# Three expert tiles of a step as one group, in the first layer of a two-layer RWKV / mixture-of-experts kernel

## The reference

```python
# s: RWKV, a recurrence over the 256 tokens of each sequence and channel
k, v, r = xk @ W_k.T, xv @ W_v.T, sigmoid(xr @ W_r.T)
wkv_t = (e1 * aa + e2 * v_t) / (e1 * bb + e2 + 1e-9)      # aa, bb, pp: carried from token to token
s = (r * wkv) @ W_o.T
# f: one of 8 experts for each token
xn  = rms_norm(x) * scale
ids = argmin(dist2(xn, centroids))
h   = xn @ up_w[e];  a, g = split(h)                       # up_w[e]: 128 x 512
y   = (a * silu(g)) @ down_w[e]                            # down_w[e]: 256 x 128
f   = where(ids == e, y, out) + x
```

## Time and profile before

| what | value |
|---|---|
| median of three runs | 1186.43 us (1185.88 to 1188.76) |
| span of the profiled execution | 1199.2 us |
| PE busy | 1061.0 us, 88% of the span |
| DVE busy | 957.6 us, 80% |
| ACT busy | 868.2 us, 72% |
| POOL busy | 789.8 us, 66% |
| DMA, mean | 89 GB/s |
| mean granted TensorE clock | 0.936 of 2.4 GHz |

### The profile page before, as it was taken

The page is one execution under the profiler, slowest core; times in us unless marked ns, Lnnn a source line. Parts: engine busy times, 40 slices in busy tenths (PEclk is TensorE's granted clock), DMA queues, the critical chain, the costliest instruction groups (busy, mean ns, idle before and its releaser), DMA issues.

```text
span 1199.2 us, 29232 instructions
## 1 busy us (share of the span) xinstructions
PE 1061.0 (88%) x8890; PEld 711.9 (59%) x8890; DVE 957.6 (80%) x2144; ACT 868.2 (72%) x2186; POOL 789.8 (66%) x1147
## 2 busy tenths in 40 slices
PE   2666369999986799999999999999999999999986
PEld 1545258898874455565555565556555565556643
DVE  6768989999994687878878887888787887888861
ACT  2555248877772488888888888888888788888874
POOL 4476678787883556776667766776677666776631
PEclk9766679999996699999999999999999999999988
DMA  9411135555552223322333233322332232323310
GB/s 258 101 39 37 34 88 162 149 156 158 143 146 67 59 69 89 86 74 66 93 79 85 65 80 82 93 68 71 90 87 73 66 89 78 90 66 77 84 33 11
DMA packets 158400, 106.17 MB, mean 89 GB/s; under 512 B 74216, under 2 KB 138408, under 8 KB 158120
## 3 DMA queue, kind: packets, MB, share of 16 engines
q1 hardware_dynamic: 154152, 95.80, 30.8%
q0 software_dynamic: 4096, 8.53, 2.5%
HBM read 72.69 MB, written 31.47 MB: 87 GB/s over the span
## 4 chain that ended last, share of the span: by engine, by line
PE 52%; issue 5%; ACT 4%; DVE 4%; DMA 2%; SPq 1%; POOL 1%; another core or an unknown queue 0%; DVEq 0%; POOLq 0%
PE PS L1956 8%; PE PS L1946 6%; PE PS L2021 5%; PE PS L1928 5%; PE PS L2043 5%; ACT PT L1802 4%; PE PS L2035 3%; DVE bm L1592 3%; PE PS L1998 3%; PE PS L2008 3%; PE PS L1898 3%; PE PS L1970 3%; PE PS L1986 3%; PE PS L2052 2%; PE PS L1906 1%
## 5 line engine op out<-in xcount | busy, mean ns | idle before, releaser
L1592 DVE TENSOR_REDUCE bm<-PS 128x16 f32<-128x1024 f32 x256 | 312.4, 1220 | 35.4 <-PE PS L1928 28.4
L1802 ACT ACTIVATE PT<-PS 128x1024 f32<-128x1024 f32 x256 | 262.0, 1024 | 23.8 <-PE PS L1946 20.4
L1956 PE MATMUL PS<-PT,rows 128*32 128x256 f32 x2048 | 138.6, 388 | 2.2 <-ACT OT L1807 2.2
L1481 POOL TENSOR_TENSOR Pr<-Pr,linv 128x512 f32<-128x512 f32 x128 | 131.6, 1039 | 5.0
L1776 ACT ACTIVATE Pr<-PS,nmf 128x256 f32<-128x256 f32 x256 | 117.1, 473 | 0.3 <-DVE nmf L1612 0.3
L1612 DVE TENSOR_REDUCE nmf<-PS 128x4 f32<-128x1024 f32 x64 | 78.4, 1225 | 46.7 <-PE PS L2021 46.7
L1946 PE MATMUL PS<-QS,KS 51*128 51x256 bf16 x1024 | 100.0, 274 | 12.3 <-ACT PT L1802 5.4
L1928 PE MATMUL PS<-KS,QS 48*128 48x256 bf16 x1024 | 101.5, 277 | 9.5 <-DVE bm L1592 6.4
L482 POOL DMA_INDIRECT xs_dram<-rows,slot x64 | 65.3, 1021 | 40.5 <-DVEq L715 22.8
L1021 PE MATMUL PS<-S,wmix 128*128 128x256 f32 x192 | 69.4, 448 | 17.7 <-DVE diff L743 16.6
L1956 PEld LDWEIGHTS PS<-PT,rows 128*32 128x32 f32 x2048 | 54.7, 109 | 46.5 <-issue 19.6
(11 more groups left out here) (253 smaller groups left out, 2822.6 us busy)
## 6 DMA issues: line engine op xcount, KB each, us to landing
up<-in_up_w SPq DMA_DIRECT2D x72, 256.0 KB, 2.9
wsel<-in_qkv_w SPq DMA_DIRECT2D x128, 96.0 KB
parts_dram<-parts SPq DMA_DIRECT2D x32, 384.0 KB
QS<-parts_dram SPq DMA_DIRECT2D x64, 96.0 KB
KS<-parts_dram SPq DMA_DIRECT2D x64, 96.0 KB
xs_dram<-zero_t SPq DMA_DIRECT2D x1, 4752.0 KB, 26.4
xs_t<-xs_dram SPq DMA_DIRECT2D x72, 66.0 KB, 2.0
ys_dram<-ys_t SPq DMA_DIRECT2D x72, 64.0 KB, 2.8
```

The source lines that it names most:

```text
L1481: pool.tensor_tensor(Pr[i][:, qt, :, :], Pr[i][:, qt, :, :], linv[:, i, qt, :].unsqueeze(2).broadcast_to([P, 2, SEQ]), ALU.mult).then_inc( ...
L1592: dve.tensor_reduce(bm[:, i // 2, :, 2 * (i % 2):2 * (i % 2) + 2, :].rearrange("p q r b -> p r q b"), bS.rearrange("p (r q b k) -> p r q b ...
L1802: act.activation(PT[i % 4][:, :, :], shifted_bank(t, i).rearrange("p (r k) -> p r k", r=2), ACT.Exp).then_inc(s_exp, 1)
L1956: last = pe.matmul(bC[j * VC:(j + 1) * VC, 0:SEQ], V2[q][:, kt, 4 * g + j, :], PT[(2 * g + j // 2) % 4][:, j % 2, kt * SEQ:(kt + 1) * SEQ] ...
```

## The change

- The three tiles of a step become one group. ACT's tanh, DVE's two multiplications, ACT's two copies and POOL's skip take all three tiles in one instruction (`128x768` in place of three times `128x256` for tanh and multiplications, `128x384` in place of three times `128x128` for the others). Only the scaling of the rows stays at one instruction a tile. Semaphores count groups, but for `s_up` and `s_upl`, which count tiles still.
- The hidden activations of a group lie in three banks of PSUM, 0 to 2, held once. The transposes of three tiles share one bank (3), the expert outputs another (4).
- The group g has `flip_tokens` on PE in step 11+g, and in step 12+g `inner` at the head of PE's list and `outer` (the products with `down_w`) at its end. The skip and the store follow in step 13+g.
- ACT's `exps` move to the head of its list from step 11 on. DVE's `denominator` moves from the end of a step to the head of the next.
- Token fetches and stores move three tiles with one DMA. `up_w` is still fetched a tile at a time into four buffers.
- SP's list of a step is written as one store, one fetch of tokens for the next step's group, and then three fetches of `up_w` for the group whose products are in the next step. The first group's `up_w` moves from ahead of step 11 into it.
- The first two sequences of the second layer are taken up a step later (`TAKE` 21 to 22).

```diff
-        xs_t = [sb(f"xs_t{i}", [P, ROW]) for i in range(G)]
+        xs_t = [sb(f"xs_t{i}", [P, TPS, ROW]) for i in range(NXS)]
...
+        psU = psU_banks.rearrange("p (i x c) -> p i x c", i=TPS, x=2)
+        psX, psY = (PS[k][:, 0:TPS * P].rearrange("p (i c) -> p i c", i=TPS) for k in (3, 4))
...
+        def group(s, k):
+            return s - FIRST - k if 0 <= s - FIRST - k < NG else None
@@ SP
-            def store(t, h, q):
-                sp.wait_ge(s_skip, t + 1)
+            def store(g):
+                sp.wait_ge(s_skip, g + 1)
...
-            def load_up(t, h, q):
+            def load_up(t):
                 after(sp, s_up, t - NUP + 1)
-                sp.load(expert_registers[q % TPS], tile_expert[0:1, bass.ds(t, 1)])
+                sp.load(expert_registers[t % TPS], tile_expert[0:1, bass.ds(t, 1)])
...
-                for turn in range(TPS):
-                    done = tile(quad, p, turn, LAST)
-                    if done:
-                        store(*done)
-                    new = tile(quad, p, turn, -3)
-                    if new and (not isinstance(new[0], int) or new[0] >= 3):
-                        load(*new)
-                    soon = tile(quad, p, turn, -1)
-                    if soon and (not isinstance(soon[0], int) or soon[0] >= 1):
-                        load_up(*soon)
+                s = number(quad, p)
+                if group(s, 2) is not None:
+                    store(group(s, 2))
+                if group(s, -1) is not None:
+                    load(group(s, -1))
+                if group(s, 0) is not None:
+                    for i in range(TPS):
+                        load_up(TPS * group(s, 0) + i)
@@ POOL
-                skip(quad, p, 0)
                 if 3 <= s < 3 + 2 * NCH:
                     scatter((s - 3) // 2, (s - 3) % 2)
-                skip(quad, p, 1)
                 first_tokens(s)
                 if runs(m[0]) and not early(m[0]):
                     products(pool, *m)
                 if runs(d[0]):
                     divide(*d)
-                skip(quad, p, 2)
+                if group(s, 2) is not None:
+                    skip(group(s, 2))
                 if runs(w[0]):
                     weigh(*w)
@@ DVE
+            def experts(g):
+                c = Chain(dve, s_gch, 1, g)
+                dve.wait_ge(s_gate, g + 1)
+                c(dve.scalar_tensor_tensor(gate[:, :, :], gate[:, :, :], 1.0, psU[:, :, 1, :], ALU.add, ALU.mult))
+                after(dve, s_dn, g)
+                dve.tensor_tensor(hid[:, :, :], psU[:, :, 0, :], gate[:, :, :], ALU.mult).then_inc(s_hid, 1)
...
+                if runs(w[0]):
+                    denominator(*w)
...
-                experts(quad, p, 0)
                 if runs(w[0]):
                     quotient(*w)
...
-                experts(quad, p, 1)
...
+                if group(s, 1) is not None:
+                    experts(group(s, 1))
                 if runs(m[0]):
                     sums(*m)
...
-                experts(quad, p, 2)
-                if runs(m[0]):
-                    if early(m[0]):
-                        products(dve, *m)
-                    denominator(*m)
+                if runs(m[0]) and early(m[0]):
+                    products(dve, *m)
@@ ACT, a step
-                experts(quad, p, 0)
+                if s >= FIRST and runs(e[0]):
+                    exps(*e)
+                if group(s, 1) is not None:
+                    gate_tanh(group(s, 1))
                 take(0)
                 if runs(r[0]):
                     receptance(*r)
+                if group(s, 0) is not None:
+                    scale_tokens(group(s, 0))
                 take(1)
                 if runs(k[0]):
                     keep(*k)
-                experts(quad, p, 1)
+                if group(s, 2) is not None:
+                    expert_out(group(s, 2))
...
@@ PE
+            def inner(g):
+                pe.wait_ge(s_xsT, g + 1)
+                after(pe, s_hid, g)
+                for i in range(TPS):
+                    t = TPS * g + i
+                    pe.wait_ge(s_upl[t % NUP], 16 * (t // NUP + 1))
                     for c in range(2 * HID // P):
...
-                transposes(quad, p, 0)
+                if group(s, 1) is not None:
+                    inner(group(s, 1))
                 take(0)
                 if runs(r[0]):
                     receptance(*r)
-                products(quad, p, 0)
-                transposes(quad, p, 1)
                 if runs(w[0]):
                     out_projection(*w)
                 take(1)
-                products(quad, p, 1)
+                if group(s, 0) is not None:
+                    flip_tokens(group(s, 0))
                 if runs(b[0]):
                     keys_values(*b)
-                transposes(quad, p, 2)
...
-                products(quad, p, 2)
+                if group(s, 1) is not None:
+                    outer(group(s, 1))
```

179 lines of the change are left out of this document (70 added, 109 removed).

## The result

The changed kernel takes 1395.96 us (median of four runs, 1392.97 to 1401.52) against 1187.58 us of the kernel before (four runs, 1185.88 to 1188.76) on the same chip: a ratio of 1.176, 95% interval 1.173 to 1.179. The prediction was 1400 us, range 1340 to 1430.

A forecast was written before the change was run, and what follows sets the result against it. A ring through SP's store and up_w fetches was to bound the first layer: 22 x (17.7 - 8.02) = 213 us, plus 1 us, on a 1199.2 us span gives 1413, less 12.8 us profile difference: 1400 us, range 1340 to 1430.

The forecast's parts named there:

- The ring and its length: First layer's expert steps: bb, POOL, skip, store, up_w fetches, products, tanh, pair close a ring; 17.7 us for 8.02.
- The terms: Parts of the ring's round from bb: store at 5.20 us, first up_w 6.58, landing 3.0, then products, tanh, pair.
- Which `up_w` sets the start: On PE, the first up_w landing at 9.58 us starts the slow products; at full clock the third, at 11.38, matters.
- the rival of 15.29 us a step: Ring closes, but PE's clock stays up or recovers at once: 1347 us; full or partly full clock 18%.
- The clock: PE idles 6.5 us a step, then starts at half clock: three tiles take 5.14 instead of 2.7 us.
- Head and tail: Around the 22 steps: PE's wait for scaled rows in the first two, a later last group; 1 us for both.
- The slower ring by contention: Fetches, store and token fetch at once make up_w's landing 4.5 us: 33 us more, 1433 us; chance 12%.
- PE's wait for scaled rows alone: Ring doesn't bind; PE's wait sets steps of 8.6 us, 8.9 with set-up work: 1206 us; chance 7%.
- The faster side: Neither ring nor wait binds; DVE sets the step with 0.48 us less: 1175 us; chance 3%.
- The Trainium skill's rule: SP's time to initiate DMAs is small: 1.38 us from store to first fetch drops out each round, giving 1370 us.

The follow-up runs named there:

- e1: Changed kernel with the store moved behind the token fetch and the three fetches of up_w in SP's list; 1205.45 us, ratio 1.011 to the kernel before.
- e2: Changed kernel with POOL's skip ahead of its three products and divide; 1328.37 us, ratio 1.113 to the kernel before.
- e4: Changed kernel with six buffers for up_w in place of four, nothing else; 1406.95 us, ratio 1.177 to the kernel before.
- e3: Changed kernel with 15 unused products of 256 columns added at the end of PE's list of a step; 1378.21 us, ratio 1.156 to the kernel before.
- b1: The kernel before run once more, unchanged, for a second profile; its second layer takes 749.3 us between first and last logits.
- e11: e9 with six buffers and SP's fetches of up_w one step earlier, for the group after next; 1183.34 us, ratio 0.9974 to the kernel before.
- e12: Changed kernel with up_w fetched one step earlier into six buffers, store still first in SP's list; 1232.47 us, ratio 1.040 to the kernel before.
- e7: e1 with ACT's scaling ahead of tanh, its exponential behind both tanhs, DVE's den addition behind the differences; 1206.32 us, ratio 1.009 to the kernel before.
- e9: e10 with DVE's multiplication to num moved behind the experts' pair; 1195.83 us, ratio 1.008 to the kernel before.
- e10: e1 with ACT's scaling ahead of tanh and DVE's den addition between scan pp and the differences; 1194.30 us, ratio 1.007 to the kernel before.

## Why the prediction was right

- **The ring and its length.** Predicted 17.7 us a step and 22 x (17.7 - 8.02) = 213 us; measured 17.70 and 213.0. e1 removes the store's place in SP's list and with it nearly all of the loss; e2 shortens the ring and keeps part of it; e4 excludes the buffers. This much is shown. That the mean agrees to the last digit is luck: 17.70 is a mean with the set-up steps, a plain step has 17.04, and my sum was made of plain steps, while the 8.02 that I took off is a mean (a plain step has 7.69). My round of 17.73 was 0.69 us too long, and the set-up work that it left out adds 0.66 us to a step in the mean; the two errors cancel.
- **The terms.** From `bb` to the store 5.06 us (5.20 by the sum; the skip is 0.99 us for 1.13). From the store to the first fetch 1.79 (1.38): 265.03 to 266.28 is 1.25, for which the earlier trace rows had 0.90. The landing 3.03 (3.0). From the products' start to tanh's 4.45 (5.30): this is the largest error, since the clock was back sooner, 3.2 us behind the start of the products, than the 4.9 us that I took from the earlier trace rows. Those rows were also a weak ground for the price of an idle time: L1040, ahead of the 5.74 us, takes 1.06 us there and 0.61 at the full clock (at 241.17), and the granted clock was 0.50 already from 105 us on. What such an idle time does is shown by the changed kernel (1.00 until 264 us, 0.50 from 266 on) and by e3. Tanh with its hand-over 0.84 (0.91), the pair with its own 1.87 (1.94). Together 17.04 against 17.73.
- **Which `up_w` sets the start.** I had the first one set the start at the slow clock, and the third set the end at the full one. In e3, at the full clock, the products start at the first landing and run through in 2.94 us: fetches and products are both 0.9 us apart, so the two come to the same. e3 is the rival of 15.29 us a step as the trace has it, 15.67.
- **The clock.** PE idles 6.81 us (6.5 predicted) and starts at half the clock; by e3 that is worth 1.4 us a step, 30 us in all. The prediction had this rival at 1347 us, 53 below the forecast; the measured difference is 28.7, for the products are only 1.5 us longer at the slow start, not 2.4.
- **Head and tail** were 1 us by the sum and are 3.1 and 1.5. The second layer, which was to keep its time, does so within what one kernel shows in two executions (753.6 and 749.3); e4 and b1 on their chips have 749.1 and 749.3.
- **The slower ring by contention** (1433 us) doesn't occur: `up_w` lands in 3.2 us at the median with the DMA share down from 0.55 to 0.24.
- **PE's wait for scaled rows alone** (1206 us) was a rival at 7%. e1 is that case, made: 8.50 us a step for the 8.6 of the rival. Its 1205.45 us are on a slower chip, so they don't confirm the 1206: by its ratio it costs 1.1%, where the rival has 1.7%, for all but its last two steps stay at 8.50 us, with set-up work too (22 steps take 185.2 us, 8.8 more than before, in place of 20). The rival's wait is in the rows of e1; its claim that the ring doesn't bind was wrong.
- **The faster side** (1175 us, DVE with 0.48 us less). e11 has no wait for `up_w` left and gets 0.26%, 3 us, not 12. What was wrong there is that DVE sets the floor: PE's own list stood at the same 7.69 us.
- **The Trainium skill's rule** (DMA: Bandwidth & Descriptors, section "Issuing engines are not separate DMA queues", initiating a DMA is usually small relative to it) would have given 1370 us. The trace of the changed kernel disagrees still more than the one before: from the store to the third fetch some 3.6 us go by (264.49, then 266.28 and two spacings of 0.9), more than the landing.

What stays open: 217.6 us were added in the first layer of these two profiles, 208.4 in the medians; e4 and b1 agree better (213.4, and 212 by e4's median). The first two profiles are a weak pair for such a sum: the span of the kernel before is 12.8 us above its median, that of the changed kernel 3.8.

## What to carry to other kernels

In a hand-written list a fetch is no earlier than the latest wait in front of it on its issuing engine. When stores and fetches are grouped, list for each wait which step's work ends it, and put what waits for this step behind the fetches of the next; then look at whether the ring still closes over two steps, for every kind of fetch (here weights and tokens). Before an engine is relieved, read from a free step whether another one's list has the same length: then there is nothing to gain.

## What the runs showed of the hardware

PE's granted clock goes down in the wait for `up_w` and comes back within the products. Windows of the changed kernel across one wait for `up_w`:

```profile
262.50:269.30 6.80, 0.00 (x1) 0.02 (x1) 3.38 (x5) 1.18 (x2) 3.13 (x4) 0.73 0.48 126
269.30:271.50 2.20, 2.19 (x10) 2.20 (x11) 0.00 (x0) 0.00 (x0) 0.00 (x0) 0.50 0.49 157
271.50:273.70 2.20, 2.20 (x17) 2.20 (x16) 0.00 (x0) 0.00 (x0) 0.00 (x0) 0.79 0.00 0
```

The granted clock is 0.50 (1.2 of 2.4 GHz) in the first half of the products and rises within the second half; the 24 products take 4.41 us in place of 2.84. Behind 3.2 us of idle time (e2) it is the same, and in e12 behind 2.5 us (at 257.39) the projections show 1.05 us in place of 0.59, at a mean granted clock of 0.57.

Two of DVE's instructions with both operands in SBUF took longer beside POOL's. The multiplication to `num` in e7, with POOL's `ev` beside it:

```profile
261.24 1.27 POOL L479 TENSOR_TENSOR ev<-ex,values 128x512 f32<-128x512 f32 x1
...
261.44 1.35 DVE L752 SCALAR_TENSOR_TENSOR num<-rtanh,num 128x256 f32<-128x256 f32 x1
```

and in e9, behind the pair, with POOL idle:

```profile
264.17 0.42 DVE L757 SCALAR_TENSOR_TENSOR num<-rtanh,num 128x256 f32<-128x256 f32 x1
```

1.35 us against 0.42 for the same instruction, and the long one ends 0.28 us behind POOL's end (262.79, 262.51); in the changed kernel it begins later beside `ev` and takes 0.64. The Trainium skill says that a DVE instruction with two inputs in SBUF and a GpSimd instruction that reads SBUF exclude each other for the whole of the one that came first (SBUF — State Buffer, section "Who interferes with whom"); the trace agrees, with these 1.35 and 0.42 us; e2's skip and `aa` (1.34 and 1.43 us for 0.99 and 0.67) show both sides paying when they are interleaved. From e10 to e9 it took DVE's busy time from 147.8 to 130.6 us of 150 (18 multiplications of 1.30 us, then 17 of 0.42). That is the end of a full DVE list; the kernel's time stayed, since the ring through `up_w` was about as long.
